# Four attention and expert layers in one program: exp of the next unit ahead of Gelu in the second expert layer, second and fourth attention begun inside the expert layers before them

## The reference, cut to what matters

```
x = x + layernorm(attn_or_ffn(layernorm(x)))     # L0_attn, L0_ffn, L1_attn, L1_ffn, L2_attn, L2_ffn, L3_attn, L3_ffn

# L0_ffn: 8 experts, 2 chosen            out = sum_e combine[t,e] * (up_e(x) * silu(gate_e(x))) @ w2_e
# L1_attn: 16 heads of 8, softmax, no mask
# L1_ffn: the last of 8 experts only
probs = softmax(xf @ Wr.T);  y = (gelu(xf @ W1[7] + b1[7]) @ W2[7] + b2[7]) * probs[:, 7:8]
# L2_attn: 16 heads, causal, polynomial instead of softmax
# L2_ffn: layer norm, a short attention over the 8 sequences, layer norm, 8 gelu experts, 2 chosen, capacity 640
# L3_attn: latent of 64, 16 query heads, one key and value head, causal softmax
latent = x @ Wc_down;  q = latent @ Wq_up;  kv = latent @ Wkv_up
# L3_ffn: 16 experts in 4 groups, 4 chosen, and a shared one
```

## Time and profile before

| | us |
|---|---|
| time before, median of 3 runs (1511.58 to 1513.2) | 1512.23 |
| profiled execution, its own time | 1508.2 |
| span of the profiled execution, first to last instruction | 1506.4 |

### The profile page before, as it was taken

How to read it: one execution, slowest core, us unless ns; L and a number is a source line. 1 busy time by engine, 2 the same in 40 slices (tenths; PEclk the granted TensorE clock), 3 DMA queues, 4 the chain that set the end, 5 groups by cost and what they waited for, 6 DMA issues and landing times.

```text
span 1506.4 us, 26816 instructions
## 1 busy us (share of the span) xinstructions
PE 1193.8 (79%) x9110; PEld 837.2 (56%) x9110; DVE 1064.8 (71%) x2986; ACT 724.5 (48%) x1182; POOL 411.6 (27%) x628
## 2 busy tenths in 40 slices
PE   5999989999958777666777874777786999977887
PEld 4666658888823333355344442666674344436776
DVE  7878766666666777445878995688864666647886
ACT  5454523333416767453666782343331466643452
POOL 4545421000023342012454542122311233100110
PEclk8999999999957999878798996799996899997999
DMA  8000000000000000000000000000000000000000
GB/s 325 1 1 1 1 1 1 0 0 0 0 1 1 2 0 1 1 1 1 1 2 0 1 2 1 1 1 1 1 1 1 1 2 0 2 1 1 1 1 29
DMA packets 5845, 14.55 MB, mean 10 GB/s; under 512 B 240, under 2 KB 4464, under 8 KB 5360
## 3 DMA queue, kind: packets, MB, share of 16 engines
q1 hardware_dynamic: 5744, 13.26, 2.3%
HBM read 12.21 MB, written 1.05 MB: 9 GB/s over the span
## 4 chain that ended last, share of the span: by engine, by line
issue 49%; PE 21%; DVE 14%; POOL 6%; ACT 4%; DVEq 4%; POOLq 3%; ACTq 0%
PE PS L1207 3%; PE PS L1155 2%; PE PS L1149 2%; PE PS L1132 2%; POOL trs L412 2%; PE PS L1377 2%; DVE mx L2021 1%; PE PS L1047 1%; POOLq L411 1%; PE PS L1024 1%; POOL hrs L412 1%; DVE w_l0f L2131 1%; DVE sbuf L1923 1%; PE PS L1113 1%; PE PS L1046 1%
## 5 line engine op out<-in xcount | busy, mean ns | idle before, releaser
L2021 DVE TENSOR_REDUCE mx<-PS 128x2 f32<-128x512 f32 (+1 forms) x256 | 155.2, 620 | 81.1 <-PE PS L1155 72.1
L715 ACT ACTIVATE w_l0f<-PS 128x512 f32<-128x512 f32 (+1 forms) x256 | 137.3, 543 | 100.8 <-PE PS L1162 98.1
L410 POOL TENSOR_TENSOR tve<-tmv,eps 128x2 f32<-128x2 f32 x64 | 14.6, 228 | 499.9 <-DVE tmv L1802 331.9
L1752 PE MATMUL PS<-hT_padded,w_l0f 128*128 128x256 f32 x512 | 121.7, 384 | 0.0
L1752 PEld LDWEIGHTS PS<-hT_padded,w_l0f 128*128 128x128 f32 x512 | 94.5, 193 | 10.7
L966 ACT ACTIVATE sg<-PS 128x512 f32<-128x512 f32 x64 | 38.2, 597 | 116.7 <-PE PS L1752 116.6
L410 POOL TENSOR_TENSOR hve<-hmv,eps 128x2 f32<-128x2 f32 x65 | 17.0, 261 | 243.2 <-DVE hmv L1786 108.8
L2950 DVE TENSOR_TENSOR y<-sg,PS 128x512 f32<-128x512 f32 x64 | 44.0, 688 | 49.7 <-ACT sg L966 42.1
L2131 DVE SCALAR_TENSOR_TENSOR w_l0f<-w_l0f 128x768 f32<-128x768 f32 x64 | 67.5, 1054 | 16.4 <-ACT w_l0f L778 15.4
L1529 PEld LDWEIGHTS PS<-w_l2f,y 128*128 128x128 f32 x512 | 71.7, 206 | 13.1 <-ACT y L831 8.7
L1529 PE MATMUL PS<-w_l2f,y 128*128 128x128 f32 x512 | 73.9, 291 | 6.2 <-ACT y L831 5.9
(11 more groups left out here) (478 smaller groups left out, 3282.9 us busy)
## 6 DMA issues: line engine op xcount, KB each, us to landing
w_l0f<-in_l0f SPq DMA_DIRECT2D x1, 3076.0 KB, 17.4
w_l2f<-in_l2f SPq DMA_DIRECT2D x1, 2214.0 KB, 18.8
w_l3f<-in_l3f SPq DMA_DIRECT2D x1, 1736.0 KB, 22.6
w_l0a<-in_l0a SPq DMA_DIRECT2D x1, 960.0 KB, 7.3
result<-X SPq DMA_DIRECT2D x1, 896.0 KB, 4.6
X<-in_x SPq DMA_DIRECT2D x1, 768.0 KB, 10.6
w_l1f<-in_l1f SPq DMA_DIRECT2D x1, 582.0 KB, 14.7
PT<-in_cbf SPq DMA_DIRECT2D x1, 576.0 KB, 8.4
```

The lines of the kernel that those rows point to most:

```text
L715: act.activation(P8[:, hh % 8, 0:width], PS[:, hh % 2, 0:width], ACT.Exp, scale=SM_SCALE).then_inc(a["pt"], 1)
L1752: ins = pe.matmul(PS[:, 2 * (c % 2) + g, b * L:(b + 1) * L], w("l0f", "w1")[:, at:at + P], hT[:], start=True, stop=True)
L2021: dve.tensor_reduce(mx[:, hh, 0:nm], PS[:, 2 + hh % 2, 0:nm * keys].rearrange("p (t k) -> p t k", t=nm), AX.X, ALU.max).then_inc(a["mx"], 1)
```

## The change

- **Second expert layer.** PE: down(i-1) comes ahead of state_transpose(i+2). ACT: gate_exp is called for unit i+1 between hidden(i) and state_copy(i+2), before it was unit i+2 and after the copy; lg and ex have two halves by parity (`half_of`). DVE: gate_max(i+1) and gate_less(i+1) open the round, gate_sum, gate_inverse and gate_parts are those of unit i, result_stats stands ahead of state_stats, and the order of drains follows. POOL: tail_rstd ahead of head_rstd. In the third attention's start PE no longer waits for the last result of this layer, and ACT does all four copies to KT and QT.
- **First expert layer and second attention.** The hardware loops end at unit 6; unit 7 is written out as unit(7, last). In it the router, exp and ranking of a next unit are left out. In their place: projection of unit 0 of the attention (`project_behind`, at c = 3, banks 6 and 7), bias and load on DVE (c = 4), the splits on POOL, the transposes of the parts on PE (at c = 6, 7, 8 and after the last down, all through bank 6), all copies on ACT, and the head of unit 1. The attention's prologue is gone.
- **Third expert layer and fourth attention.** Units 6 and 7 take in the heads of units 0 and 1 of the attention, `down_behind`, `latent_behind`, `up_behind`, `load_behind`, the splits on POOL and the transposes and copies of the parts. The own head and the prologue are gone. For all units the head's transpose and the router stand one expert later on PE, inner_transpose and short_qkv one up later; on ACT state_copy, inner_copy and short_load stand one expert later; on DVE gate_max and gate_less come after combine(2) (before: after combine(1)), and the rest of the ranking and the value products are interleaved anew, with one drain more.

The diff, cut to its core (indentation shortened; the order is POOL, ACT, PE, DVE):

```diff
     if there(i + 2):
         all_value_products(i + 2)
+    if i == NB - 2:
+        head_rstd(head0[L3_ATTN] + 1)
     tail_rstd(i + (tail0[l] + 1))
     if there(i + 2):
         head_rstd(i + (head0[l] + 4))
+    if i == NB - 2:
+        head_rstd(head0[L3_ATTN] + 2)
+        pool.wait_ge(AT[L3_ATTN]["ld"], LOADS[L3_ATTN])
+        pool.sem_inc(pool_turn, 1)
+        split_keys(pool, L3_ATTN)
+        split_queries(pool, L3_ATTN, 0)
 continue
...
 with pool.Fori(0, NB - 1) as i:
     tail_rstd(i + (tail0[l] + 1))
     head_rstd(i + (head0[l] + 3))
+head_rstd(head0[L1_ATTN] + 2)
+pool.wait_ge(AT[L1_ATTN]["ld"], LOADS[L1_ATTN])
+pool.sem_inc(pool_turn, 1)
+split_keys(pool, L1_ATTN)
+split_queries(pool, L1_ATTN, 0)
 tail_rstd(NB + tail0[l])
...
 gate_exp(0)
 state_copy(1)
-gate_exp(1)
 for i in range(NB):
     hidden(i)
+    if there(i + 1):
+        gate_exp(i + 1)
     state_copy(i + 2)
-    if there(i + 2):
-        gate_exp(i + 2)
...
 for i in range(NB):
     up(i, 1)
     down(i, 0)
-    if there(i + 1):
-        head_transpose(l, i + 1)
+    if i == NB - 1:
+        up_behind()
     up(i, 2)
     down(i, 1)
     if there(i + 1):
-        router(i + 1)
+        head_transpose(l, i + 1)
     up(i, 3)
     down(i, 2)
+    if there(i + 1):
+        router(i + 1)
     up(i, 4)
     down(i, 3)
+    if i >= NB - 2:
+        state_behind(i - (NB - 2))
     up(i, 5)
     down(i, 4)
+    up(i, 6)
     if there(i + 3):
         inner_transpose(i + 3)
-    up(i, 6)
     down(i, 5)
+    up(i, 7)
     if there(i + 3):
         short_qkv(i + 3)
-    up(i, 7)
     if there(i + 1):
         earlier(i + 1)
     down(i, 6)
+    if i == NB - 2:
+        down_behind()
+    if i == NB - 1:
+        pe.wait_ge(behind["qs"], 1)
+        parts_behind(QS, range(0, half), 1)
+        pe.wait_ge(behind["ks"], 1)
+        parts_behind(KS, range(1), 3)
     if there(i + 2):
         short_transpose(i + 2)
     if there(i + 1):
         up(i + 1, 0)
     down(i, 7)
+    if i == NB - 1:
+        parts_behind(QS, range(half, 2 * half), 6)
     if there(i + 2):
         short_project(i + 2)
...
 router(1)
 for i in range(NB):
     up(i)
+    if there(i - 1):
+        down(i - 1)
     if i < NB - 1:
         state_transpose(i + 2)
-    if there(i - 1):
-        down(i - 1)
     if there(i + 2):
         router(i + 2)
...
         if c == HEAD_AT:
             head_transpose(l, i)
-        if c == ROUTE_AT:
+        if c == ROUTE_AT and last:
+            project_behind()
+        elif c == ROUTE_AT:
             pe.wait_ge(f["hn"], i + 1)
             router(hN)
+        if c == 6 and last:
+            pe.wait_ge(behind["ks"], 1)
+            parts_behind(KS, range(0, half))
+        if c == 7 and last:
+            pe.wait_ge(behind["kq"], 1)
+            parts_behind(KS, range(half, 2 * half))
+            head_transpose(l, i + 1)
+        if c == 8 and last:
+            pe.wait_ge(behind["kq"], 2)
+            pe.wait_ge(behind["qs"], 1)
+            parts_behind(QS, range(0, half))
         if c >= 1:
             down(c - 1)
+unit_ready(0)
+router(hT)
+with pe.Fori(0, NB - 1) as i:
+    unit(i, False)
+unit(NB - 1, True)
...
         maximum_parts(1, 1 - par)
-dve.wait_ge(w_in[name], 16)
-dve.wait_ge(second_sets, 1)
-head_stats(X, 1)
-load_qkv(0, 0, 0, 6)
-if l == L1_ATTN:
-    load_qkv(0, 1, 0)
-dve.drain()
-split_keys(dve, l)
-split_queries(dve, l, 0)
-head_norm(X, 1, head0[l] + 2)
-parts_copy(ntr - 2, KT[:, 0:1] if l == L3_ATTN else KT[:, half:], 3)
-parts_copy(ntr - 1, QT[:, half:], 1)
 iterations(dve, l, one)
...
         outer_moments()
     combine(i, 0)
+    if i == NB - 2:
+        head_stats(X, 0)
+    if i == NB - 1:
+        load_behind()
+        head_norm(X, 1, head0[L3_ATTN] + 2)
     if S:
         short_scores(s)
     dve.drain()
     combine(i, 1)
     if S:
         short_max(s)
+    dve.drain()
+    if S:
+        short_less_max(s)
+    if N:
+        hidden_state(n)
+    dve.drain()
+    combine(i, 2)
+    if i == NB - 2:
+        head_norm(X, 0, head0[L3_ATTN] + 1)
+    if N:
+        inner_stats(n)
...
-dve.drain()
-gate_parts(0)
-gate_max(1)
-dve.drain()
-gate_less(1)
 for i in range(NB + 1):
     t, g, s, n = i - 1, i + 1, i + 2, i + 3
     if s == NB + 1:
         load_behind()
+    if there(g):
+        gate_max(g)
     if s <= NB + 1:
         head_norm(X, s % NB, s + (head0[l] + 1))
+    dve.drain()
+    if there(g):
+        gate_less(g)
     if there(t):
         result(t)
     dve.drain()
     if there(t):
         result_share(t)
+    dve.drain()
+    if there(t):
+        result_stats()
+    if there(i):
+        gate_sum(i)
+    dve.drain()
+    if there(t):
+        result_moments()
+    if there(i):
+        gate_inverse()
+    dve.drain()
+    if there(i):
+        gate_parts(i)
     if n <= NB + 1:
         state_stats(n)
     dve.drain()
-    if there(t):
-        result_stats()
     if n <= NB + 1:
         state_moments()
-    dve.drain()
-    if there(t):
-        result_moments()
-    if there(g):
-        gate_sum(g)
-    dve.drain()
-    if there(g):
-        gate_inverse()
-    if there(s):
-        gate_max(s)
-    dve.drain()
-    if there(g):
-        gate_parts(g)
-    if there(s):
-        gate_less(s)
-    dve.drain()
     if there(t):
         result_norm(t)
         dve.drain()
         result_add(t)
-        dve.drain()
+    dve.drain()
...
+                head_stats(X, 1)
+            if c == 4:
+                load_behind()
+            if c == 5:
+                head_norm(X, 1, head0[L1_ATTN] + 2)
     combine(i, E8 - 1)
     dve.drain()
     tail_stats(acc)
-    if more:
+    if not last:
         head_stats(X, (i + 2) % NB)
         gated(i + 1, 0)
-    top_rank(cwn[:, :, 0:E8], E8, 2, cwn[:, :, 0:E8], rank[:, :, 0:E8])
-    take_shares()
+        top_rank(cwn[:, :, 0:E8], E8, 2, cwn[:, :, 0:E8], rank[:, :, 0:E8])
+        take_shares()
     tail_add(l, i, acc)
 head_stats(X, 1)
 gated(0, 0)
 with dve.Fori(0, NB - 1) as i:
-    unit(i, i + 1, True)
-unit(NB - 1, 0, False)
+    unit(i, i + 1, False)
+dve.wait_ge(w_in["l1a"], 16)
+unit(NB - 1, 0, True)
...
```

More of the change, by code:

```diff
@@ L864, in _ @@
                             hidden(i, c)
-                            if c == 1 and there(i + 1):
+                            if c == 2 and there(i + 1):
                                 state_copy(i + 1)
@@ L876, in _ @@
                                 short_copy(i + 2)
+                            if i == NB - 2 and c == 5:
+                                state_behind(0, oT[:])
+                            if i == NB - 2 and c == 7:
+                                latent_behind()
+                            if i == NB - 1 and c == 4:
+                                state_behind(1, hT)
+                    parts_behind(0, QT[:, 0:half], 1)
+                    parts_behind(1, KT[:, 0:1], 3)
+                    parts_behind(2, QT[:, half:], 6)
                 elif l == L3_FFN:
@@ L959, in gate_exp, with parts_behind, unit @@
                         act.activation(ex[:, :, 0:E8], lg[:, :, 0:E8], ACT.Exp).then_inc(f["gx"], 1)
-                    gate_exp(0)
-                    warm(ACT.Silu)
-                    with act.Fori(0, NB) as i:
+                    behind, half = AT[L1_ATTN], NH // 4
+                    def parts_behind(n, dst):
+                        act.wait_ge(behind["tr"], n + 1)
+                        act.activation(dst, PSB[:, 6, :].rearrange("p (a b) -> p a b", b=L), ACT.Copy)\
+                           .then_inc(behind["kq"], 1)
+                    def unit(i, last):
                         for c in range(E8):
@@ L1533, in down, with state_behind, down_behind, up_behind @@
                         ins.then_inc(f["o"], 1)
+                    behind, half = AT[L3_ATTN], NH // 4
+                    def state_behind(u):
+                        pe.wait_ge(hd_h, u + (head0[L3_ATTN] + 1))
+                        for t in range(T):
+                            ins = pe.transpose(TR[:, t * P:(t + 1) * P], h[:, t, :], ident)
+                        ins.then_inc(hd_tr, 1)
+                    def down_behind():
+                        pe.wait_ge(w_in["l3a"], 16)
+                        pe.wait_ge(hd_hT, head0[L3_ATTN] + 1)
+                        pe.matmul(PS[0:64, 1, 0:L], w("l3a", "down"), oT[:], start=True, stop=True)\
+                          .then_inc(behind["lat"], 1)
+                    def up_behind():
+                        pe.wait_ge(behind["lats"], 1)
+                        for t in range(T):
+                            n = D + 2 * HD
+                            ins = pe.matmul(PS[:, 3, t * n:(t + 1) * n], latT[:, t * P:(t + 1) * P],
+                                            w("l3a", "up")[0:64], start=True, stop=True)
+                        ins.then_inc(behind["qkv"], 1)
+                    def parts_behind(src, pairs, bank):
+                        for b, pair in enumerate(pairs):
+                            for t in range(T):
```

(33 more changed lines are left out.)

161 lines of the change are left out of this document (78 added, 83 removed).

## The result

The changed kernel takes 1471.12 us, median of 4 runs (1467.46 to 1472.04), against 1511.9 for the kernel before (1508.97 to 1513.2, 4 runs): ratio 0.973, 95% interval 0.9716 to 0.9743. The forecast was 1468.5 with a range of 1459 to 1486. The profiled execution took 1471.18 us, 37.0 less than the one of before (1508.2; that one lay 4 us under its median).

A forecast was written before the change was run, and what follows sets the result against it. No engine was taken to bound the whole; each stretch has its own limit. Gains of 10.9 + 17.5 + 1.5 + 13.8 = 43.7 us off the median 1512.2 gave 1468.5, range 1459 to 1486.

The forecast's parts named there:

- First expert layer into second attention: Seam from the first expert layer's end to the second attention's first maximum: at 422.9 instead of 433.83, gain 10.9 us.
- The rule on the shared port: First seam: DVE and GpSimd lock a shared SBUF port pair; splits half as long again put keys 1.8 us later, gain about 8.
- the prediction's first condition: Shared SBUF port: DVE takes the exclusive lock when it has two SBUF inputs; the other condition was its 2-port mode.
- Second expert layer: Loop and seam into the third attention: period 6.0 us, closed by ACT and PE with exp after Gelu; gain 17.5 us.
- Third expert layer: Units 0 to 5: DVE is what lasts, so a gain of 1.5 us in all, bounds -6 to +6.
- its one PE-made wait, 1.43 us at combine(7), hangs on short_transpose and stays: Third expert layer, middle units: DVE's only wait made by PE, 1.43 us, was to stay unchanged.
- a sign that the prediction gave for being wrong: Third expert layer: units longer by 2 us and more would show the forecast wrong.
- rival D: Third expert layer: gate chain, some 12 us, exposed behind combine(2); slower than before, 1517 at 7 us a unit; chance 0.04.
- Third expert layer into fourth attention: Units 6 and 7 to the fourth attention's first maximum: last `down` 2.8 us later, including 1.0 of waiting; gain 13.8 us.
- A: Second expert layer: the clock does not hold, only the seam's 3.2 us stays; 1483 us, chance 0.17 together with C.
- C: Second expert layer: loop stays closed through DVE, period 8.7 us kept; 1483 us, chance 0.17 counted with A.
- B: Both attention seams: POOL's splits or bank 6 not hidden, each seam gives 5.5 us less; 1480 us, chance 0.14.

## Why the prediction was right, and where not

- **First expert layer into second attention.** Forecast 10.9, read 10.2; in this execution unit 7 began 1.5 us later than in the one of before (402.21 against 400.72), so the seam itself gave 11.7. PE's wait for the keys was to be 1.7 and is 1.75; the last `down` was to end 4.2 later and ends 3.5 later from the unit's start (eight transposes push PE's next step back by 0.45 us, not by 0.6); the first maximum was to come 3.9 behind it and comes 3.93. The terms stand.
- **The rule on the shared port.** POOL's splits took 3.64 and 3.62 us beside DVE's gated products and combines, and 3.7 and 3.6 in the earlier trace rows. The keys were not 1.8 us late, and the gain was not 8. The trace does not bear out a stretching of both splits by half. The products and sums read one input from PSUM, so they don't have the two SBUF inputs of the prediction's first condition. The one DVE step beside the splits with its input in SBUF is the norm of two tiles, and it was longer: 0.73 us at 410.95, and 1.22 at 440.52 in the kernel before, against 0.60 in the layer's other units. If anything waited, it was DVE; no run separates this from other causes.
- **Second expert layer.** Forecast 17.5 with the seam, read 17.0. Period 6.0 forecast, 5.9 read at full clock; last `up` at 682.89, where 689.9 less the 7.5 us that came from upstream gives 682.4; first round to be 1.6 worse, 1.2 read. The clock held in part: 1.00 was granted in units 1, 2, 5 and 6, 0.87 and 0.88 in units 3 and 4, and 0.83 over the layer with its slow start and end, against 0.79 before. The failed step is the reason: the sum let the period follow from the exp standing right behind Gelu. The runs show that PE's `down` ahead of the transposes gives nearly all of it alone (84.0 to 67.2 us). The exp ahead gives 8.1 us alone (84.0 to 75.9) and at most 0.8 on top of the swap: ACT's 3.28 us of standing with the table loaded and PE's 4.03 belong to one loop, and the two gains don't add up.
- **Third expert layer.** Here the forecast was wrong: 1.5 us of gain, 4.0 of loss in the profiled pair. The step that failed is "its one PE-made wait, 1.43 us at combine(7), hangs on short_transpose and stays". The price from the row was one at full clock; the steps ahead of the wait run at either clock, and the wait is 1.4 or 3.3 us with it. The trace of the kernel before already had both: unit 5 of it (shown above), one after the row that the forecast went by, has `up` and `down` at 1.2 GHz and the long wait. DVE's busy time in unit 4 did not change (23.5 us before, 23.3 after), so nothing was wrong with its round. The bound of +-6 held the loss, but a sign that the prediction gave for being wrong did come: unit 4 is 2.2 us longer (27.0, now 29.2), where the middle units were to stay within 1 us of 25.6. The mechanism of rival D, a gate chain exposed, is not what happened: `earlier` does wait for it 1.92 us, but covered by useless matmuls the same wait costs nothing.
- **Third expert layer into fourth attention.** Forecast 13.8, read 15.0: counted from X of unit 6, the last `down` ends 1.6 us later than before, not 2.8, and the maximum follows 3.88 behind it, as forecast. The term that was too large is the 1.0 us of waiting: PE's rows of unit 7 show no such wait.
- **Rivals.** A and C gave 1483; the layer's 66.4 us rule both out. B gave 1480; the waits for POOL in the last units of the first and third expert layers are 1.75 us and none, and PE waits 0.17 and 1.12 us for ACT's copies at the end of the first. Two figures of the working don't hold: the low end of the range should be 1460.5 (the layer's 1.5 us are in the 1468.5 already), and the 12 us of rival D's chain stand in no row.

## What to carry to other kernels

A wait that stands ahead of independent work in an engine's queue is the first thing to move: here the swap of two steps on PE gave 16.8 us of a layer, and the rest of the rework of that loop at most 0.8 on top. Of two idle times in one loop ask which is the cause and which waits for the same closing; undoing each edit alone tells it. Price a chain of matmuls on the critical path at both clocks when a gap of PE stands ahead of it, and read the clock of each unit, not of the layer. What an edit gives in its own layer can be given back in layers that nobody touched.

## What the runs showed of the hardware

- Useless work can shorten a kernel's layer: 14 fp32 matmul instructions of 128x256 more in each of five units brought the third expert layer to 221.5 us twice; the six profiled executions with the same order and without that work had 222.8 to 226.2, five of them 224.9 and more.
- The same `up`, `down` and transposes took 1.4 us of DVE's waiting at full clock and 3.3 at 1.2 GHz. Two executions of one program differ in where the clock falls: units 5 and 6 of the second attention took 19.2 and 14.3 us in one execution of the kernel before (granted clock 1.00 in both) and 20.6 and 15.9 in the other (0.91 and 0.94).
- An activation table load took 1.28 us each time, in all kernels. Behind Gelu's end at 666.58 it started at 666.60, and the exp at 667.89.
